# Experts in 71 tiles; the next attention's weights and first row numbers fetched during them; matmuls between the two stages

## The reference, cut to what matters

```
x = x + attn0(layernorm(x))          # 16 heads of 8, causal
x = x + xattn0(layernorm(x), ctx)    # cross attention, 16 heads of 8
x = x + experts(layernorm(x))        # 8 experts, each token goes to its 2 best
x = x + attn1(layernorm(x))          # "wide": 16 heads of 64, rotary, causal
x = x + xattn1(layernorm(x), ctx, mask)
x = x + ffn(layernorm(x))            # fake-quantised feed-forward, width 352

experts:
  logits = x @ router_w.T + router_b;  topv, topi = top_k(logits, 2);  gates = softmax(topv)
  out = sum over e of  gate_e * ( silu(x @ gate_w[e].T) * (x @ up_w[e].T) ) @ down_w[e].T
```

## Time and profile before

| | us |
|---|---|
| median of 3 runs | 1147.18 (1140.87 to 4976.68) |
| the profiled execution | 1146.26 |
| its span, first to last instruction | 1144.5 |
| expert stage, first gate matmul to last down matmul | 380.4 to 587.9 |
| from there to the first instruction of wide attention | 587.9 to 590.9 |
| first matmul of wide attention | 604.5 |

### The profile page before, as it was taken

One profiled execution on the slowest core, in us unless ns is written; L12 is line 12 of the kernel. 1 busy time (PEld: TensorE's weight loads), 2 busy tenths in 40 slices (PEclk: granted clock), 3 DMA queues, 4 the chain that ended last, 5 costly groups with the idle time before them and its releaser, 6 DMA issues. The chain is left out here.

```text
span 1144.5 us, 38720 instructions
## 1 busy us (share of the span) xinstructions
PE 988.8 (86%) x14758; PEld 800.5 (70%) x14759; DVE 840.3 (73%) x2013; ACT 585.6 (51%) x1014; POOL 586.9 (51%) x735
## 2 busy tenths in 40 slices
PE   5999999999955699999956999999999999868554
PEld 2666666666642699999954888888888888746213
DVE  4878787888839244444426999999999999658696
ACT  3665656677630466666622444444444444446465
POOL 4232424344300433333225888888888886626534
PEclk9999999999965799999987999999999999965585
DMA  8200000100000111111230000000000000041002
GB/s 256 103 2 0 2 11 13 28 20 28 11 28 0 36 48 46 48 48 46 44 111 13 15 13 12 9 11 11 11 9 11 11 11 1 1 112 57 1 1 74
DMA packets 36985, 37.61 MB, mean 33 GB/s; under 512 B 7142, under 2 KB 31145, under 8 KB 36522
## 3 DMA queue, kind: packets, MB, share of 16 engines
q1 hardware_dynamic: 31690, 27.33, 8.0%
q0 software_dynamic: 4352, 8.92, 3.1%
q10 hardware_dynamic: 866, 0.33, 0.1%
HBM read 27.65 MB, written 8.91 MB: 32 GB/s over the span
## 5 line engine op out<-in xcount | busy, mean ns | idle before, releaser
L1283 POOL DMA_INDIRECT e_x<-xn_rows,e_where x72 | 68.4, 950 | 166.5 <-DVE e_where L1264 118.4
L360 POOL TENSOR_SCALAR n_KX<-n_KT,n_of_head 128x512 f32<-128x512 f32 x124 | 84.2, 702 | 121.8 <-ACT n_KT L601 85.0
L1253 DVE COPY e_y<-e_Y_ps 128x128 f32<-128x128 f32 x72 | 21.0, 292 | 112.3 <-PE e_Y_ps L1220 112.3
L760 DVE TENSOR_REDUCE n_row_max<-n_S_ps 128x16 f32<-128x1024 f32 x64 | 78.2, 1221 | 27.0 <-PE n_S_ps L451 27.0
L1440 POOL TENSOR_TENSOR a_E<-a_E,a_rsum 128x512 f32<-128x512 f32 x64 | 66.7, 1042 | 56.2 <-DVE a_rsum L1804 56.2
L665 ACT ACTIVATE n_ET<-n_ET_ps 128x1024 f32<-128x1024 f32 x64 | 65.5, 1024 | 46.4 <-PE n_ET_ps L461 45.6
L461 PEld LDWEIGHTS n_ET_ps<-ident,n_E 128*128 128x128 f32 x512 | 57.1, 142 | 34.9 <-issue 20.1
L764 DVE TENSOR_TENSOR n_E<-n_S_ps,n_row_max 128x1024 f32<-128x1024 f32 x64 | 78.4, 1225 | 2.9
L1210 PE MATMUL e_G_ps<-e_xT,e_gate_here 128*128 128x128 f32 x576 | 78.2, 280 | 0.5 <-ACT e_up_here L1173 0.5
L1220 PE MATMUL e_Y_ps<-m_down_w,e_hT 128*128 x576 | 76.3, 275 | 1.6 <-issue 1.4
L1688 ACT ACTIVATE a_OT<-a_VQ_ps 128x512 f32<-128x512 f32 x64 | 38.2, 598 | 77.0 <-PE a_VQ_ps L1584 77.0
(11 more groups left out here) (282 smaller groups left out, 2686.8 us busy)
## 6 DMA issues: line engine op xcount, KB each, us to landing
slot_out<-e_y SPq DMA_DIRECT2D x72, 64.0 KB
X<-in_x SPq DMA_DIRECT2D x8, 256.0 KB, 5.3
n_ctxT<-in_ctxT SPq DMA_DIRECT2D x8, 256.0 KB, 3.1
m_gate_w<-in_L_ffn_gate_w SPq DMA_DIRECT2D x1, 2048.0 KB, 7.9
m_up_w<-in_L_ffn_up_w SPq DMA_DIRECT2D x1, 2048.0 KB, 13.7
m_down_w<-in_L_ffn_down_w SPq DMA_DIRECT2D x1, 2048.0 KB, 18.0
xn_rows<-n_xn SPq DMA_DIRECT2D x8, 256.0 KB
t_ctxT<-in_ctxT SPq DMA_DIRECT2D x8, 256.0 KB
```

Of the source, the lines that this page charges most:

```text
L360: last = nc.gpsimd.tensor_scalar(KX[:, p, :, h * T:(h + 1) * T], src, of_head[:, h:h + 1], 1.0, ALU.mult, ALU.mult)
L760: nc.vector.tensor_reduce(row_max[:, u % 2, :], src, AX.X, ALU.max).then_inc(max_done, 1)
L1283: nc.gpsimd.indirect_dma_start(out=x[:, j, :], out_offset=None, in_=k.xn_rows, in_offset=bass.IndirectOffsetOnAxis(ap=where[:, j, :], axis ...
```

## The change

- `NT` is 71 instead of 72, also in `slot_out` and in the table of tile numbers; `tile_hot` has rows of 71.
- `tiles` loops over 48 tiles in 6 turns and writes out the last 15.
- The seven loads move from SP's program in wide attention to SP's program in the experts, behind the store of tile 7. The buffers and the semaphore `wide_in` are made before the first phase.
- ACT fills `where` for units 0 to 3 at the end of its program in the experts.
- The gathers stay where they were, in POOL's prologue of wide attention (now through a helper).
- PE issues 36 matmuls of 128x128 bfloat16 on the identity behind its last down product, and 90 more as the first thing of wide attention. Nothing reads their results.

```diff
+def keep_warm(nc, k, bank, count):
+    for _ in range(count):
+        nc.tensor.matmul(bank, k.identb[:], k.identb[:], start=True, stop=True)
...
+def gather_expert_rows(nc, k, p, i, u):
+    nc.gpsimd.indirect_dma_start(
+        out=k.expert_rows[:, p, i, u, :], out_offset=None, in_=k.slot_out,
+        in_offset=bass.IndirectOffsetOnAxis(ap=k.where[:, p, i, u:u + 1], axis=0)).then_inc(k.got[p][i], 16)
...
-    NT = 2 * NU + NE
+    NT = 2 * NU + NE - 1
...
+    LOOPED = NT // Q * Q - Q
...
-            with eng.Fori(1, NT // Q - 1) as i:
+            with eng.Fori(1, LOOPED // Q) as i:
                 for j in range(Q):
                     body(i * Q + j, j, NT)
-            for j in range(Q):
-                body(NT - Q + j, j, Q - j)
+            for t in range(LOOPED, NT):
+                body(t, t % Q, NT - t)
...
                 sp.dma_start(k.slot_out[bass.ds(t * P, P), :], y[:, p, :]).then_inc(stored[p], 16)
+                if isinstance(t, int) and t == Q - 1:
+                    for dst, name in k.wide_constants:
+                        sp.dma_start(dst[:], k.d[name]).then_inc(k.wide_in, 16)
...
             tiles(act, body)
+            for nb in range(2):
+                nc.scalar.activation(k.where[:, nb], k.slots[:, :, nb * 2:nb * 2 + 2], ACT.Copy).then_inc(k.where_ready, 1)
...
-            down(NT - 1, Q - 1, expert_of(NT - 1))
+            down(NT - 1, (NT - 1) % Q, expert_of(NT - 1))
+            keep_warm(nc, k, xT_ps[:, P:2 * P], 36)
...
-        @block.sync
-        def _(sp):
-            for dst, name in [(wq, "L1_attn_wq"), (wk, "L1_attn_wk"), (cos, "c_cos"), (sin, "c_sin"), (wv, "L1_attn_wv"),
-                              (wo, "L1_attn_wo"), (bias_row, "L1_attn_bo")]:
-                sp.dma_start(dst[:], d[name]).then_inc(weights, 16)
...
             def prologue():
-                pe.wait_ge(weights, 16 * N_WEIGHTS)
+                keep_warm(nc, k, Y_ps[:, 0:P], 90)
+                pe.wait_ge(k.wide_in, 16 * len(k.wide_constants))
                 transpose_x(0)
...
             def prologue():
-                slots_of(0, 0)
-                slots_of(1, 1)
                 normalise(0)
                 slots_of(2, 0)
```

More of the change, by code:

```diff
@@ L870, in _, with prepare_wide_attention, sb @@
             run(dve, prologue, step, epilogue)
+def prepare_wide_attention(nc, k, ctx):
+    def sb(name, shape, dt=F32):
+        return ctx.enter_context(nc.sbuf_tensor(f"a1_{name}", shape, dt))
+    k.wide_wq = sb("wq", [P, 4, 2, P])
+    k.wide_wk = sb("wk", [P, 4, 2, P])
+    k.wide_wv = sb("wv", [P, 4, 256])
+    k.wide_wo = sb("wo", [P, 4, 2, C])
+    k.wide_bias_row = sb("bias_row", [P, C])
+    k.wide_cos = sb("cos", [P, T])
+    k.wide_sin = sb("sin", [P, T])
+    k.where = sb("where", [P, 2, 2, 2], I32)
+    k.expert_rows = sb("expert_rows", [P, 2, 2, 2, C])
+    k.wide_constants = [(k.wide_wq, "L1_attn_wq"), (k.wide_wk, "L1_attn_wk"), (k.wide_cos, "c_cos"), (k.wide_sin, "c_sin"),
+                        (k.wide_wv, "L1_attn_wv"), (k.wide_wo, "L1_attn_wo"), (k.wide_bias_row, "L1_attn_bo")]
+    k.wide_in = nc.alloc_semaphore("a1_wide_in")
+    k.where_ready = nc.alloc_semaphore("a1_where_ready")
+    k.got = [[nc.alloc_semaphore(f"a1_got{p}{i}") for i in range(2)] for p in range(2)]
+def gather_expert_rows(nc, k, p, i, u):
+    nc.gpsimd.indirect_dma_start(
+        out=k.expert_rows[:, p, i, u, :], out_offset=None, in_=k.slot_out,
+        in_offset=bass.IndirectOffsetOnAxis(ap=k.where[:, p, i, u:u + 1], axis=0)).then_inc(k.got[p][i], 16)
 def prepare_mixture(nc, k, ctx):
@@ L1275, in _ @@
             tiles(dve, body)
-            output(NT - 1, 1)
+            output(NT - 1, (NT - 1) % 2)
         @block.gpsimd
@@ L1311, in sem @@
             return nc.alloc_semaphore(f"{n}_{name}")
[L1313 to L1321, removed]
+        where, expert_rows, where_ready, got = k.where, k.expert_rows, k.where_ready, k.got
+        wq, wk, wv, wo, bias_row, cos, sin = k.wide_wq, k.wide_wk, k.wide_wv, k.wide_wo, k.wide_bias_row, k.wide_cos, k.wide_sin
         stats = sb("stats", [P, UB, 6])
@@ L1455, in gather @@
                     wait_here(pool, where_ready, nb + 1, passed)
-                nc.gpsimd.indirect_dma_start(
-                    out=expert_rows[:, p, i, u, :], out_offset=None, in_=k.slot_out,
-                    in_offset=bass.IndirectOffsetOnAxis(ap=where[:, p, i, u:u + 1], axis=0)).then_inc(got[p][i], 16)
+                gather_expert_rows(nc, k, p, i, u)
             def prologue():
@@ L2637, in constants @@
         "c_part_no": np.arange(P, dtype=np.float32)[:, None],
-        "c_tile_no": np.tile(np.arange(2 * NU + 8), (P, 1)).astype(np.float16),
+        "c_tile_no": np.tile(np.arange(2 * NU + 7), (P, 1)).astype(np.float16),
         "c_row_no": np.tile(np.arange(P), (P, 1)).astype(np.float16),
```

17 lines of the change are left out of this document (7 added, 10 removed).

## The result

| | median, us | runs | profiled execution | its span | granted clock |
|---|---|---|---|---|---|
| before, on the same chip | 1145.24 | 6 (one of them 4976.68) | 1146.26 | 1144.5 | 0.913 |
| changed | 1135.26 | 6 (1134.39 to 1137.3) | 1134.39 | 1132.6 | 0.919 |

The ratio is 0.9932, with a 95% interval of 0.9912 to 0.9952: 7.8 us less (5.5 to 10.1), where I had forecast 4.4. The change stays within 2%, as forecast. On the profiled execution that I had summed against, the ratio makes 1138.5, inside the range.

The account below looks back on a forecast made before the run. The prediction took the experts as PE-bound, followed by a start-up chain without PE where POOL is busiest. Its terms, -2.9 and -1.5, summed to -4.4 against the profiled 1146.26, giving 1141.8 us, with a range of 1136 to 1148.

Parts of the forecast that it names:

- One tile and one turn: PE-bound experts: one tile less saves 2.79 and one loop turn less 0.15, together -2.9 us.
- Row numbers and loads away from the start: Start of wide attention: earlier first gather and faster landing let POOL's power start sooner, -1.5 us (gain 0.8 to 3.0).
- Loads in the experts: SP's seven loads behind tile 7's store: tile 8's store lands in time for tile 10's copy, 0 (up to +1.5).
- PE idling in tiles 9 to 14: Experts: a sign named in advance that would show the prediction wrong; no size or chance given.
- 36 matmuls: Ahead of the barrier: they take 2.2 us and PE arrives when SP does, so 0; barrier 2.1 later if 0.12 apart.
- 90 matmuls: Behind the barrier: they take 5.4 us, PE then idles 6.7, half clock at the transposes, so 0.
- My price of 2.4 for a full clock: First transposes: if the clock stayed full, PE's work there would take half, a gain of 2.4 us; rival's chance 0.12.
- `tile_hot` with 71 columns: DVE's 64 plan instructions in the experts: one column less and odd rows change nothing, 0; outer end +6.2 us.
- the odd rows: Rival in `tile_hot`: rows at odd two-byte multiples cost DVE its packed mode, +3.1 us, 1144.9; chance 0.08.
- The second dip of the clock: Rival in wide attention: the half clock from 620.0 to 626.9 goes, up to -2.3 us, 1139.5; chance 0.10.
- the matmuls 0.12 apart: Rival: barrier 2.1 later, but the 90 last 10.8 and the clock stays full, -2.4 us, 1141.5; chance 0.08.
- the slower case: Rival on SP's queue in the experts: stores wait behind loads at half speed, +9.2 us, 1151.0; chance 0.05.

Follow-up runs that it names:

- e9: Kernel before with 85 inert matmuls at the head of PE's wide attention, moving only PE's code by 170 instructions; ratio to before 0.9967.
- e10: Kernel before with 128 inert matmuls at the head of PE's wide attention, moving only PE's code by 256 instructions; ratio to before 0.9995.
- e11: Changed kernel without the 36 matmuls ahead of the barrier and with 57 instead of 90 behind it; ratio to the kernel before 0.9950.
- e5: Kernel before, still 72 tiles, with the last 16 written out behind the loop instead of 8; ratio to before 0.9964.
- e7: Changed kernel with the seven loads spread, one behind each store of tiles 1 to 7; ratio to the kernel before 0.9930.
- e3: Changed kernel without the 36 and the 90 inert matmuls; ratio to the kernel before 0.9944.
- e4: Changed kernel with 205 instead of 90 matmuls behind the barrier; ratio to the kernel before 0.9931.
- e12: Changed kernel with loads spread behind stores 1 to 7, POOL's first power after the fourth gather, 45 and 190 matmuls around the barrier; 1130.09 us, 0.9878 of before.
- e2: Kernel before with 71 tiles only (48 looped, 15 written out); loads, row numbers and PE's matmuls as before; ratio to before 0.9940.

## Why the prediction was right in its direction and short by 3.4

The step that failed is the sum itself: it held only terms at the places that the diff touches. It took for granted that code which the change does not touch takes the same time, and never listed what moves when code ahead of it gets longer. That term was worth -5.3, more than the whole forecast.

- *Left out: the place of PE's code.* Seven more tiles written out and 126 inert matmuls shifted PE's wide attention within its blocks. -5.3 in the profiled executions (403.5 to 398.2). Some 4 of it are shown to be the place of PE's code, by e9 and e10, and by e11 in the other direction; e5 shows 4.4 with all 72 tiles. What the remaining 1.2 hang on is open. That PE stood still because its next block was not there is my reading: one round of wide attention is 128 matmuls with a weight load each, 256 instructions, so successive rounds meet the edge of a block at about the same place; 104 of these matmuls (L1584, L1552, L1560) run in 1.64 us (665.09 to 666.73), while a packet of q8 precedes the end of a pause by some 2.5 (665.4 to 667.96). No row names the wait.
- *One tile and one turn.* Forecast -2.9, measured -2.79 (174.89 to 172.10). The turn is worth nothing: the pitch of 2.94 stands ahead of the copy of tile 7 alone, where the loop is entered, in every kernel, and the later turns are at 2.79. I had read the entry of the loop and taken it for every turn.
- *Row numbers and loads away from the start.* Forecast -1.5, bounds -0.8 and -3.0; measured -1.1. The chain was right link by link: variance 1.57 ahead (forecast 1.7), the power behind the eighth gather. The gap of 0.30 ahead of the first gather was 0.73.
- *Loads in the experts.* Forecast 0, bound 1.5; measured +1.0 (e7 takes it away, others show 0.5 to 1.0). I had the store's landing at 423 on the old clock, and it is 419.85 + 3.79 = 423.6, 3.79 being the shift of tile 7 (413.06 to 409.27). I took DVE's 1.64 of idle for the cushion; the copy was 2.2 late and PE lost 1.0, so the cushion was 1.2. In e3 and e4 the copy is 1.9 and 1.7 late and PE loses 0.7 and 0.5, which gives 1.2 again. PE idling in tiles 9 to 14 was one of my signs of being wrong, and it came.
- *36 matmuls.* Forecast 2.2 and PE no later than SP; measured 2.17, and 584.4 against 585.1. But the barrier grew by 0.6. In the five kernels with 72 tiles it is 2.96 each time; in those with 71 tiles 2.86 to 3.50 without matmuls ahead of it and 3.45 to 3.83 with them. In the changed kernel SP is still last at the barrier (585.1), behind its last store; what made the barrier longer is open.
- *90 matmuls.* Forecast 5.4, a pause of 6.7, half clock; measured 5.18, 7.3, half clock. My price of 2.4 for a full clock was measured as 1.5 (e4, with the longer stretch of half clock behind it) and 2.5 (e12, with the early power in it too).
- *`tile_hot` with 71 columns.* Forecast 0, measured 0. In the profiled execution of the changed kernel the records grow while the plan runs, but those of `row_hot` beside them, whose shape did not change, grow as well. The timeline of DVE after, early and late:

```profile
349.97 0.30 DVE L1113 TENSOR_SCALAR p_tile_hot<-m_tile_no,p_tile_f,m_token_no 128x71 f16<-128x71 f16 x1
350.17 0.25 DVE L1112 TENSOR_SCALAR p_row_hot<-m_row_no,p_row_f 128x128 f16<-128x128 f16 x1
...
371.81 0.34 DVE L1113 TENSOR_SCALAR p_tile_hot<-m_tile_no,p_tile_f,m_token_no 128x71 f16<-128x71 f16 x1
372.01 0.29 DVE L1112 TENSOR_SCALAR p_row_hot<-m_row_no,p_row_f 128x128 f16<-128x128 f16 x1
```

The pitch of the pair stays 0.37 throughout, as before. In e2, with the same 71 columns, nothing grows (ns, min/median/max; the earlier trace rows has 297/303/309 for 72 columns):

```profile
L1079 DVE TENSOR_SCALAR p_tile_hot<-m_tile_no,p_tile_f,m_token_no x64: 298/302/305, 351.3 to 374.6; 128x71 f16<-128x71 f16 x64
```

So neither the odd rows nor the column less cost anything; what lengthened the records in that one execution is not shown, and it did not lengthen the pace. The Trainium skill, "VectorE: DVE Perf Modes", section "Mode 2×_1P — pack two bf16 into one 32-bit read", asks for 4-byte alignment, by which I had worked out 1.8: the traces don't bear that out. The Trainium skill, "Vector Engine (DVE) Microarchitecture Reference", section 5.1, says that 4-byte alignment makes no difference: the traces agree.
- *The second dip of the clock* stayed in the changed kernel (0.51 from 613.9 to 620.8); that rival fell. So did the matmuls 0.12 apart (190 took 10.77), the odd rows and the slower case: the store behind the loads landed at 423.6 on the old clock, not at 427.5 or later.

The known terms make -2.8 - 1.1 + 1.0 + 0.6 = -2.3 instead of -4.4, and with -5.3 for the place -7.6, beside -7.8 by the ratio. Without the unforeseen term the forecast would have missed by 2.1 on the other side. Two errors of opposite sign met, and the range held the time by luck: I had stretched its low end for gains of the clock, which did not come, and the time went there for another reason. The two profiled executions themselves are 11.9 apart. Beside these 7.6, 1.8 lie ahead of the first copy of `y`, 2.0 are the pause in the first tile that comes and goes, and 0.5 lie behind wide attention.

## What to carry to other kernels

When a change makes an engine's code longer or shorter, list the "issue" pauses of that engine in the code behind it, and keep a gain and a loss of their sum in the range; they are not constants. To judge a change of under one per cent, run beside it the kernel before with its code shifted: here that control, by 170 instructions that do no useful work, was worth 3.8 of the 7.8 us. Cushions are measured between the wait and the engine that sets the pace, not as the idle time of the engine that waits.

## What the runs showed of the hardware

- PE's code comes in packets of about 16 KB on a queue of its own, whose count followed PE's instructions from 47 to 51. Around a loop of small matmuls PE stood still four times for 0.55 to 1.78 us, 4.1 to 4.7 us in one execution. Moving only PE's code took it away (170 instructions) or left it (256). The Trainium skill, "Runtime: NRT & Kernel Launch", section "Instruction fetch mechanics", gives blocks of 16 KiB, 256 instructions; the packets' size and count and e10 agree. It also calls the cost of crossing such an edge mostly hidden; the pauses of up to 1.78 us do not agree with that for this loop. And it says that a taken branch to a target outside the present window of two pages forces a fetch. A turn of this loop has 516 matmuls with nearly as many weight loads (700.00 to 724.08), some 1030 instructions and so more than two blocks, and q8 moved nothing from 672.6 to 989 while it turned: for PE this trace does not agree. The pauses stand in the first turn and behind the end, where q8 does move packets.
- After 5.18 us of matmuls and a pause of 7.3 the clock was at half when the transposes came. After 11.61 us and a pause of 0.9, and after 10.77 us and a pause of 0.29, it was full. No run lies between. Either way a stretch at half clock followed, beginning 12.1 to 15.5 us behind the first transposes: 6.8 us long in the changed kernel and in e12, 10.1 in e4.
- A store issued right behind seven loads of 2.2 MB landed 5.0 us after its issue (414.79 to about 419.8, when the copy that waited for it began); with one load behind each store no copy waited.
